# Key and value projections of a decoder layer: whole fp32 products in place of three split products

## The reference

```python
q = jnp.einsum('bse,ae->bsa', query, Wq) + bq
k = jnp.einsum('bse,ae->bsa', key, Wk) + bk      # key = value = context, 1601 x 256
v = jnp.einsum('bse,ae->bsa', value, Wv) + bv
scores = jnp.einsum('bqa,bka->bqk', q, k) / scale
scores = jnp.where(mask == 0, jnp.float32(-10000000000.0), scores)
attn = jax.nn.softmax(scores, axis=-1)
return jnp.einsum('bqk,bka->bqa', attn, v)
```

## Time and profile before

| | us |
|---|---|
| three runs | 853.4, 848.8, 852.02; median 852.02 |
| profiled execution, device time | 850.47 |
| its span in the trace | 848.6 |
| TensorE busy (matmul) | 657.9 of 848.6 (78%) |
| VectorE busy | 610.2 (72%) |
| ScalarE busy | 416.3 (49%) |
| mean granted TensorE clock | 0.864 of 2.4 GHz |

### The profile page before, as it was taken

The page is one execution under the profiler, slowest core; times in us unless marked ns, Lnnn a source line. Parts: engine busy times, 40 slices in busy tenths (PEclk is TensorE's granted clock), DMA queues, the critical chain, the costliest instruction groups (busy, mean ns, idle before and its releaser), DMA issues. The chain is left out here.

```text
span 848.6 us, 11256 instructions
## 1 busy us (share of the span) xinstructions
PE 657.9 (78%) x3308; PEld 424.5 (50%) x3308; DVE 610.2 (72%) x1034; ACT 416.3 (49%) x742; POOL 453.8 (53%) x324
## 2 busy tenths in 40 slices
PE   5559866996599784653389799999999989699950
PEld 2123212341134220210048699998989978588840
DVE  3937868898979899897987467668687583454316
ACT  3447688668856897554425333433334221144420
POOL 1218759987979799985941212212333137136560
PEclk9789977998889976565579999999999899799985
DMA  7043332343333433464202122322413039655418
GB/s 189 7 103 90 85 79 69 95 103 83 84 90 94 100 91 95 97 184 103 66 7 78 39 78 94 123 75 93 140 52 102 14 94 304 172 140 150 138 28 296
DMA packets 70586, 87.45 MB, mean 103 GB/s; under 512 B 18197, under 2 KB 47320, under 8 KB 70526
## 3 DMA queue, kind: packets, MB, share of 16 engines
q1 hardware_dynamic: 55166, 67.78, 30.1%
q10 hardware_dynamic: 11616, 10.76, 3.9%
q0 software_dynamic: 3744, 8.19, 2.7%
HBM read 36.54 MB, written 18.66 MB: 65 GB/s over the span
## 5 line engine op out<-in xcount | busy, mean ns | idle before, releaser
L257 POOL TENSOR_TENSOR b_in<-u_rep,b_rep 128x1024 f32<-128x1024 f32 x128 | 298.7, 2357 | 74.9 <-DMA dt_rep<-dt 41.3
L466 DVE TENSOR_TENSOR_SCAN h<-ps,hlast,b_in 128x512 f32<-128x512 f32 x256 | 306.4, 1263 | 43.3 <-ACT ps L374 33.2
L374 ACT ACTIVATE ps<-dt_rep,neg_a 128x512 f32<-128x512 f32 x256 | 170.7, 684 | 71.7 <-DVE h L466 60.7
L604 PE MATMUL ps<-h,pick 128*32 128x512 f32 x512 | 84.9, 746 | 45.5 <-DVE h L466 45.4
L501 PE MATMUL ps<-xnT,w_in 128*128 128x512 f32 x128 | 68.7, 683 | 13.0 <-ACT xnT L303 8.7
L909 POOL DMA_INDIRECT rows_by_token<-yt,yrow x46 | 44.7, 972 | 55.0 <-DVE yrow L1282 27.8
L604 PEld LDWEIGHTS ps<-h,pick 128*32 128x32 f32 x512 | 11.3, 118 | 110.7 <-DVE h L466 99.1
L1063 DVE TENSOR_TENSOR p_lo<-ps,p_hi 128x512 fp32r<-128x512 f32 x64 | 35.1, 586 | 40.3 <-ACT p_hi L920 40.1
L1320 PE MATMUL ps<-v_hi,p_hi 128*128 128x256 f32 x208 | 60.4, 290 | 1.2 <-DVE x_res L1176 1.2
L1320 PE MATMUL ps<-v_lo,p_hi 128*128 128x256 f32 x208 | 59.0, 284 | 0.0
L1320 PE MATMUL ps<-v_hi,p_lo 128*128 128x256 f32 x208 | 59.0, 284 | 0.0
(11 more groups left out here) (248 smaller groups left out, 1377.5 us busy)
## 6 DMA issues: line engine op xcount, KB each, us to landing
u_rep<-u SPq DMA_DIRECT2D x256, 64.0 KB, 2.0
dt_rep<-dt SPq DMA_DIRECT2D x256, 64.0 KB, 2.0
mask_sb<-in_mask_BxSxS_ik_dram SPq DMA_DIRECT2D x16, 800.5 KB, 4.3
xt<-rows_by_expert SPq DMA_DIRECT2D x46, 129.0 KB, 2.4
rows_by_token<-pad ACTq DMA_DIRECT2D x4, 1024.0 KB, 5.1
yb<-rows_by_token SPq DMA_DIRECT2D x4, 512.0 KB, 4.6
yb<-rows_by_token ACTq DMA_DIRECT2D x4, 512.0 KB, 5.7
x_res<-in_x_dram SPq DMA_DIRECT2D x1, 1536.0 KB, 8.6
```

Source lines behind the costliest of these rows:

```text
L257: pool.tensor_tensor(b_in[:, (t - 1) % NB:(t - 1) % NB + 2, :], u_rep[:, n % 2, j - 1:j + 1, :], b_rep[:, q % 2, g, :].unsqueeze(1).to_bro ...
L374: act.activation(psA[:, t % NDA, :], dt_rep[:, n % 2, j, :], ACT.Exp, scale=neg_a[:, k:k + 1]).then_inc(exp_ready, 1)
L466: dve.tensor_tensor_scan(h[:, QC * (s % NH) + j, :], psA[:, t % NDA, :], b_in[:, t % NB, :], hlast[:, k:k + 1], ALU.mult, ALU.add).then_in ...
L604: last = pe.matmul(psY[32 * j:32 * j + 32, :], pick[:, :], h[:, QC * (s % NH) + j, :], start=False, stop=(g == NG - 1))
```

## The change

The context and the weights Wk and Wv are evacuated once, as plain fp32 tiles (`cT`, `wkT`, `wvT`), by ScalarE alone. Keys and values are multiplied in whole fp32, with one matmul instruction in place of three. The keys and values themselves are still split into high and low when they leave PSUM. The waits on `prep_lo` are renumbered by `halved`, which counts only items that have a low part, and TensorE waits for ScalarE's copies of the context (`prep_hi`) where it waited for the low parts. `moments` stands where it stood in the list of items, but VectorE has nothing to do ahead of it now.

```diff
-                c_hi, c_lo = sb("c_hi", [P, KE, SKP], F32R, prep), sb("c_lo", [P, KE, SKP], F32R, prep)
-                wk_hi, wk_lo = sb("wk_hi", [P, KE, DM], F32R, prep), sb("wk_lo", [P, KE, DM], F32R, prep)
-                wv_hi, wv_lo = sb("wv_hi", [P, KE, DM], F32R, prep), sb("wv_lo", [P, KE, DM], F32R, prep)
+                cT, wkT, wvT = sb("cT", [P, KE, SKP], F32, prep), sb("wkT", [P, KE, DM], F32, prep), sb("wvT", [P, KE, DM], F32, prep)
...
-        wkv_items = [(bank[n].rearrange("p (k n) -> p k n", k=KE), hi[:, :, :], lo[:, :, :], None)
-                     for n, (hi, lo) in ((1, (wk_hi, wk_lo)), (2, (wv_hi, wv_lo)))]
-        ctx_items = [(bank[(3 + n) % 8][:, 0:b - a], c_hi[:, k, a:b], c_lo[:, k, a:b], None)
+        wkv_items = [(bank[n].rearrange("p (k n) -> p k n", k=KE), dst[:, :, :], None, None) for n, dst in ((1, wkT), (2, wvT))]
+        ctx_items = [(bank[(3 + n) % 8][:, 0:b - a], cT[:, k, a:b], None, None)
...
+        def halved(n):
+            return len([lo for _, _, lo, _ in items[:n + 1] if lo is not None])
...
             for n, (src, hi, lo, bias) in enumerate(items):
+                if n == 3 + len(ctx_items):
+                    moments()
                 if lo is None:
                     continue
-                if n == 3 + len(ctx_items):
-                    moments()
...
                     pe.wait_ge(prep_hi, before[-1] + 1)
-                    if before[-1] > 0:
-                        pe.wait_ge(prep_lo, before[-1])
+                    if halved(before[-1]):
+                        pe.wait_ge(prep_lo, halved(before[-1]))
...
             for g, (a, b) in enumerate(KCOL):
-                pe.wait_ge(prep_lo, 2 + KE * (g + 1))
+                pe.wait_ge(prep_hi, 3 + KE * (g + 1))
                 for m in range(KE):
                     out_ = take()
                     for k in range(KE):
-                        last = products(out_, (wk_hi[:, k, m * P:(m + 1) * P], wk_lo[:, k, m * P:(m + 1) * P]),
-                                        (c_hi[:, k, a:b], c_lo[:, k, a:b]), k == 0, k == KE - 1)
+                        last = pe.matmul(out_, wkT[:, k, m * P:(m + 1) * P], cT[:, k, a:b], start=(k == 0), stop=(k == KE - 1))
                     last.then_inc(prep_ps, 1)
...
                 for k in range(KE):
-                    last = products(out_, (c_hi[:, k, c * P:(c + 1) * P], c_lo[:, k, c * P:(c + 1) * P]),
-                                    (wv_hi[:, k, :], wv_lo[:, k, :]), k == 0, k == KE - 1)
+                    last = pe.matmul(out_, cT[:, k, c * P:(c + 1) * P], wvT[:, k, :], start=(k == 0), stop=(k == KE - 1))
                 last.then_inc(prep_ps, 1)
             pe.wait_ge(prep_hi, len(items))
-            pe.wait_ge(prep_lo, len(items) - 1)
+            pe.wait_ge(prep_lo, halved(len(items)))
```

More of the change, by code:

```diff
@@ L869, in _ @@
             pool.wait_ge(b_in, 48)
-            pool.wait_ge(prep_lo, len(items) - 1)
+            pool.wait_ge(prep_lo, halved(len(items)))
             pool.wait_ge(prep_ps, len(items))
@@ L1476, in _ @@
                     pe.wait_ge(prep_hi, q_last + 1)
-                    pe.wait_ge(prep_lo, q_last)
+                    if halved(q_last):
+                        pe.wait_ge(prep_lo, halved(q_last))
                     step(-2)
```

## The result

| | before | after |
|---|---|---|
| median, lowest to highest | 851.74 us (847.95 to 855.76, 11 runs) | 856.02 us (852.93 to 858.3, 11 runs) |
| ratio | | 1.0049, 95% interval 1.0029 to 1.0069 |
| profiled execution, span | 848.6 us | 854.8 us |
| TensorE busy | 657.9 us, 3308 rows | 663.3 us, 3266 rows |
| VectorE busy | 610.2 us | 605.4 us |

The changed kernel is slower by 4.2 us (2.5 to 5.9). The interval excludes no change at all, but it holds the mark of 0.5% (4.3 us), so whether the difference is under or over that mark is not settled. The forecast was 855.5 us, +3.6 us. VectorE lost 4.8 us of work and it bought almost nothing. TensorE gained 5.4 us of busy time with 42 rows less: 3.35 us of it lie in the 33 us of the program that the change touches (29.90 us busy against 26.55), the rest in parts whose code is the same in both kernels.

What follows compares the result with a forecast made beforehand. TensorE's stream was taken to bound both product stages; keys +1.7 and values +1.9 us made +3.6, on the median 852.02 giving 855.6, stated as 855.5 us. Range 853.8 to 857.2, or 852.3 to 858.3 with both clock cases.

Steps and rivals of the forecast that it cites:

- TensorE's stream bounds both stages: Key and value products: a longer TensorE stream moves the end one for one; keys' matmuls add 2.01 us, values' 1.9.
- The price of a whole fp32 matmul: Key and value products: 0.858 us against 0.69 for three fp32r at 512 columns, 0.432 against 0.359 at 256.
- four passes against three: Key and value products: a whole fp32 matmul passes four times over the columns, split products three; a quarter to third more stream.
- The single wait before the keys: Before the first key product: without the wait for VectorE's low part of the context, 0.23 us gained.
- the 0.1 us that I had kept as a bound: First key matmul after the gap: about 0.1 us longer than its neighbours, so the start's gain is 0.2 to 0.35 us.
- The chain behind the keys: After the last large key product: ScalarE's copy and three k_lo on VectorE last as before, closing up by at most 0.1 us.
- The small keys' gain of 0.4 us: Four key products of 128 columns: about 1.0 us where twelve ran 1.4; the gain does not reach the chain.
- Moments: VectorE's moments run right behind the barrier, 7 us earlier, GpSimd's inverse deviation follows; nothing gained.
- The price of the stretch: First query tile's Wq product and first nine value matmuls: TensorE's lower clock costs 1.6 us in all, kept unchanged.
- Its two rivals: TensorE's lower clock around the first query tile: one more such period, 857.2 us, chance 0.14; or none, 854.0 us, chance 0.13.
- The rest of the way to the end: Behind the loop's first scores: nothing runs ahead by itself, so the +3.6 us goes through to the end undiminished.
- The other side: Both product stages, rival: one whole fp32 matmul goes as one row, not two; -7.1 us, 844.9 us, chance 0.03.

Runs made afterwards that it cites:

- both_keep_low: Kernel before with whole fp32 matmuls for keys and values, VectorE's ten low-part subtractions and TensorE's wait for them kept; ratio to before 1.006 (1.0038 to 1.0083).
- keys_whole: Kernel before with only the keys' split products replaced by whole fp32 matmuls, all low parts still made; 853.98 against 851.68 us, ratio 1.0024.
- before_lead_split: Kernel before with first query tile's transposes two value items later, its Wq product one item behind them; 849.43 against 850.9 us, ratio 0.9979.
- four_products: Kernel before with a fourth split product, low by low, in keys and values; timed 6.9 us slower than before, ratio 1.0081 (1.0053 to 1.0109).

## Why the prediction was right

**TensorE's stream bounds both stages.** Shown. Each part alone came through with 2.0 us for an addition of 1.9 to 2.0, with VectorE's work untouched. In the changed kernel's window of the keys VectorE's busy time is 2.63 us of 9.60, where it was 8.96, and TensorE is busy for all of it in both:

```profile
448.40:458.00 9.60, 9.60 (x35) 5.06 (x34) 2.63 (x4) 5.62 (x12) 4.23 (x10) 1.00 0.45 171
```

**The price of a whole fp32 matmul.** Shown, by 24 rows of 592 ns and 52 of 379, with two rows for each matmul. Of the 2.4 GHz clock's periods, the 0.432 us of a matmul of 256 columns are 1037, or 4.05 for each column, and the 0.1197 us of an fp32r row are 287, or 1.12. That is the sense of "four passes against three" here; what TensorE does within one fp32 matmul no row shows. The prediction said in words that the change adds a quarter to a third to the stream; its own pitches give 24% for 512 columns and 20% for 256, and its sum uses the pitches.

**The single wait before the keys.** 0.23 us forecast, 0.23 measured, and the 0.1 us that I had kept as a bound was there too.

**The chain behind the keys.** The three k_lo took 1.27 us where they took 1.32. TensorE's idle before the lead went from 1.26 to 1.60 us, forecast from 1.3 to 1.7. The small keys' gain of 0.4 us fell into this idle, as the step said; where the lead is split it came out, 3.15 us between the kernels in place of 3.62.

**Moments.** GpSimd's inverse deviations, which follow the moments, were ready at 451.70 us and the row tile that needs them started at 462.24; nothing waited. No run isolates the move, but in both_keep_low the moments are in their old place, and the 0.33 us that it loses up to the lead are accounted for by the wait and the first row.

```profile
448.77 2.93 POOL L856 TENSOR_TENSOR attn_rstd<-attn_rstd,attn_powers 128x16 f32<-128x16 f32 x1
```

**The clock.** The price of the stretch, 1.6 us forecast, measured 1.57. Its two rivals had chances of 0.14 and 0.13; in six profiles of the two kernels neither happened. But in both_keep_low, whose TensorE list and idles at the lead are those of the changed kernel, the stretch stayed away, so that rival was a real one.

**The rest of the way to the end.** The forecast let 3.6 us go through undiminished, and the timed difference was 4.2 us (2.5 to 5.9): the two agree within the interval. That the forecast's 855.5 us lies 0.5 us from the measured 856.02 is in part luck: the median of the kernel before moved from 852.02 to 851.74 us with more runs, and the timed difference came out 0.6 us larger than the forecast's. The spans of the profiles are further apart: 850.0 us before and 856.2 changed in the mean of three, 6.2 us. Of these 3.7 lie in the distance, 1.4 behind it (377.7 against 376.3) and 1.1 ahead of the barrier (445.6 against 444.4). Behind the distance each kernel's own spread is larger, 2.3 and 2.4 us. Ahead of the barrier the three profiles of either kernel do not overlap (443.97 to 444.81 and 445.50 to 445.66), but the changed kernel with the lead later or split, whose code is the same there, has 444.80 and 444.36. Over all 14 profiles of this case the part behind averages 378.0 us in the eight with whole fp32 products and 377.9 in the six without, so nothing there goes with the form of the product. The part ahead averages 444.9 and 444.4. Why the parts outside the distance differ from one execution to the next stays open; no experiment was aimed at it.

**The range.** The bounds that the prediction names, 1.2 and 0.2 us, give 854.1 to 856.9 and not 853.8 to 857.2. The result lies inside both.

**The other side.** One row per matmul would have given 26.2 us for keys_whole; it is refuted by all kernels above. The Trainium skill, Perfetto Trace Analysis, section Engine Utilization, halves the array's output rate for FP32_LOW_HIGH in a footnote, which would give the same if it were the price of a matmul. The trace agrees with half the rate for each of the two rows only (0.216 us for 256 columns, 2.02 clock periods for each); the matmul is at a quarter.

## What to carry to other kernels

Count passes and not instructions: three fp32r products took 0.69 us at 512 columns and 0.36 at 256, one whole fp32 matmul 0.86 and 0.43, so on an engine that sets the end the split products are the cheaper ones, until the columns are so few that each row costs the same (128 columns here: three rows of 0.11 us against two). Work taken from an engine that is busy but waits for nothing on the chain gives what the chain's one wait for it lasts, 0.3 us here for 4.8 us of busy time. Where the chain leaves the bounding engine for a detour over others, put independent work of that engine into the detour. That shortened the distance by 3.6 us with split products and by 4.0 with whole ones, as much as the product's form is worth (3.2 to 3.6), though the timed gain of the first was only 1.8 us (0.2 to 3.4).

## What the runs showed of the hardware

A row of fp32r with 128 columns has a pitch of 0.11 us in a stream (key rows of before_lead_split, 457.94, 458.06, 458.17, 458.28 and so on), and so has a row of whole fp32 with 128 columns (in the changed kernel's keys six in 0.83 us, the last 0.275 long, so 0.111 each), though at 256 and 512 columns the whole fp32 row takes nearly twice as long as the fp32r row (0.216 against 0.120, 0.429 against 0.230). The loop's rows of 66 columns are 0.11 apart as well. Each of these rows has a weight load of its own (PEld), and the loads are 0.11 us apart too:

```profile
457.89 0.22 PE L1322 MATMUL ps<-c_hi,wk_hi 128*128 128x128 f32 x1
457.94 0.28 PE L1322 MATMUL ps<-c_lo,wk_hi 128*128 128x128 f32 x1
458.06 0.27 PE L1322 MATMUL ps<-c_hi,wk_lo 128*128 128x128 f32 x1
...
458.00 0.19 PEld L1322 LDWEIGHTS ps<-c_hi,wk_lo 128*128 128x128 f32 x1
458.11 0.19 PEld L1322 LDWEIGHTS ps<-c_hi,wk_hi 128*128 128x128 f32 x1
...
460.36 0.83 PE L1471 MATMUL ps<-cT,wkT 128*128 128x128 f32 x6
```

The first small row behind the large ones is followed after only 0.05 us (457.89 to 457.94). So it may be the load and not the row that costs 0.11 us; no run separates the two.

Two idles of 1.3 to 1.6 and 0.47 us, with two transposes between them, were followed by a fall of TensorE's clock from 2.4 to 1.2 GHz in eight of the ten profiles that had both idles; both_keep_low and four_products had them too and stayed at full clock. The fall does not come in the idles themselves: in the second profile of the kernel before TensorE was busy again from 460.87 and kept a clock of 0.99 up to 462.00. In the four profiles in which these idles were filled or shortened the clock was 1.00 throughout. So filling them went with the full clock each time, and the idles are not shown to be the whole cause.
